# A new issue order for every engine in an attention and mixture-of-experts kernel on one core

## The chip, the core and the metric

The kernel runs on one core of a Trainium2 chip. The metric is device microseconds of one execution, less is better. Times are medians of runs; the trace is of one profiled execution.

## What is computed

The input `x` has 32 sequences of 128 tokens with 128 features. One cross-attention layer and one mixture-of-experts feed-forward layer follow each other. In float32, cut to what matters:

```
xn = layernorm(x); q, k, v = xn@wq+bq, ctx@wk+bk, ctx@wv+bv          # 16 heads of 8
o = (q @ k.T / sqrt(8)) @ v          # linear: no softmax over tokens
x1 = x + softmax(o, over each head's 8 features) @ wo.T + bo
t = rmsnorm(layernorm(x1)) * norm_w
weights = the 2 best of softmax(t @ gate.T) among 8 experts, scaled to sum 1
h1[e] = t@w1.T + 2*(t@a1[e].T)@b1[e].T;  h3[e] the same with w3, a3, b3  # rank 16
act[e] = silu(h1[e]) * h3[e]                                             # 512 wide
out[e] = act[e]@w2.T + 2*(act[e]@a2[e].T)@b2[e].T
result = x1 + sum over the 2 experts of weight * out[e]
```

## The kernel before, in words

**Tiling.** The 32 sequences are cut into 8 blocks (0 to 7, `LAST` is 7) of 4 sequences, 512 tokens. Features lie on the 128 partitions, tokens on the 512 columns. The three stages of the pipeline overlap: while the feed-forward part of block b runs, the attention of block b+2 and the residual, norm and gate of block b+1 are computed between its matmuls, and block b-1 is finished and stored. The 8 experts' low-rank matrices are stacked to 128 rows (8 x 16), and a token's expert is chosen by multiplying with a 0/1 mask, so no token is moved.

**Precision.** Most products of the feed-forward part are split: each operand is a rounded high half (`_hi`, written by ScalarE) and the difference (`_lo`, written by VectorE or GpSimd), and three matmuls (high x high, high x low, low x high) replace one.

**The work of block b, by engine.** TensorE: `hidden(b, n)` for n = 0 to 7 (L628) makes the hidden layer, 128 of its 512 features at a time; even pairs (n = 0, 1, 4, 5) compute the base product (L603) and the first expert's addition (L617) in the two banks h1 and h3, 12 matmuls; the others (2, 3, 6, 7) add the second expert's difference on top, 6 matmuls. The banks are h1[n%2] and h3[n%2] and are free once ScalarE's silu and VectorE's product have read them (L585). `a2_product` (L638) and `w2_product` (L663) are the down projections, 3 matmuls for each of 4 chunks; k=1 accumulates in b_ps from the second expert's activation (`b_split`), k=0 in z_ps from the weighted sum of both (`z_split`). `lora_in(b+1, s)` (L572) makes u for the next block, in the banks h3[0] and h3[1]. `b2_product(b-1)` (L686) and `tail(b-1)` (L696) end the block before. `turn_...` are transposes; with `project`, `queries`, `keys_times_values`, `attention_out` and `gate` they are plain float32.

ScalarE: `silu_step(b, n)`, the high halves (`b_high`, `z_high`, `um_high`, `v_high`, `ctx_high`), the normalisations of x and x1 (`normal_x`, `normal_tok`), copies out of PSUM and the exponentials. silu and exp need different tables, so each block has two table loads.

VectorE: `act_step(b, n)` (L1291, silu x h3, from SBUF and PSUM), residual, moments, softmax pieces (`sum_exp`, L1174), the choice of experts (`top_logits`, `choose`, L1214), then at the end of a block a long run: `scale_last`, `total(2)`, `total(3)`, `b_low` and `z_low` of chunks 2 and 3, the two masks of the next block, `mask_u(b+1, 0)` and `(b+1, 1)` (u x mask, L1276, from PSUM), `um_low(b+1)` (L1286), `first_weight` (L1257: `den`, then a reciprocal), `v_part` twice.

GpSimd: the larger low halves and additions of chunks 0 and 1 (`scale_step`, `total_first`, `b_low`, `z_low`, 1.3 to 2.4 us each), `um_low(b+1)` of the difference (L1608), `norm_heads` (L1601), `scale_mask`, `v_sum`, `v_low`, and the inverse square roots (`rstd_x`, `rstd_x1`, four short operations each with a power in them).

**What sets the order.** Nothing but the written order: each engine has a list of calls for the first block, one for the loop `for b in range(1, LAST)` and one for the last block (L724 on for TensorE, L990 on for ScalarE, L1400 on for VectorE, L1648 on for GpSimd), and every call waits on semaphores for what it needs. Engines execute in order, so a call that waits holds everything behind it. The choice of experts goes through DRAM: `spread_choice` (L399) on the SyncE queue writes `choice` out and reads it back spread over all partitions as `chosen`, on which the masks depend. At the block boundary `hidden(b, 0)` needs, in this order, `um_hi` of the first expert, `um_low(b)` by VectorE for its third lora matmul, and the first of `mask_u(b, 1)` before it may write h3[0].

Lines of work that the change leaves as they are keep all instructions, shapes and buffers; so do the DMA issues of the SyncE queue.

## Time and profile before

| | |
|---|---|
| median of 3 runs | 325.44 us (325.4 to 326.32) |
| the profiled execution | 322.72 us, of which its span is 320.9 us |
| busy: TensorE, VectorE, ScalarE, GpSimd | 92%, 73%, 59%, 59% of the span |
| TensorE clock granted | full speed in 39 of 40 slices, 0.6 in the last |
| start of blocks 1, 2, 3 on TensorE | 69.20, 105.92, 141.82 us |
| start of blocks 6, 7, and the end | 249.51, 283.23, 320.9 us |

A "block" here starts at the first matmul of `hidden(b, 0)` on TensorE. Blocks 2 to 5 take 35.9 us each. Matmul durations in the trace overlap: a 128x512 matmul of a split product lasts 0.39 us but the next starts 0.23 us later, so it is the distance of starts that counts. The median of the timed runs is 2.7 us above the profiled execution.

### The profile page before, as it was taken

How to read it: one execution, taken by the hardware profiler on the slowest of the kernel's cores; microseconds unless marked ns; L12 is line 12 of the kernel's file. 1: busy time of each engine (PE TensorE's matmuls, PEld its weight loads, DVE VectorE, ACT ScalarE, POOL GpSimd, SP SyncE). 2: the span in 40 equal slices, each digit the busy share in tenths (PEclk: the TensorE clock that was granted, in tenths of full speed). 3: DMA queues.
4: the chain of work that ended last, by engine and by line, in shares of the span. 5: the costliest groups of instructions: out<-in, count | busy, mean ns of one | idle time of the engine just before them, and what ended most of it. 6: DMA issues, size and time to landing. Idle time of an engine off the chain costs nothing.

```text
span 320.9 us, 4516 instructions
## 1 busy us (share of the span) xinstructions
PE 294.3 (92%) x1485; PEld 237.1 (74%) x1485; DVE 233.7 (73%) x621; ACT 187.9 (59%) x309; POOL 188.5 (59%) x171
## 2 busy tenths in 40 slices
PE   6768999879999999999999999999999979996993
PEld 5545778658788778878788778878888767885782
DVE  3879877695679766895679767895579766973364
ACT  2456956358657577448657576548647455654511
POOL 3472469727981589527981689527941688136910
PEclk9999999999999999999999999999999999999996
DMA  5720020200201021200211020200010000200000
GB/s 166 260 66 2 1 67 0 100 0 3 98 21 79 0 66 35 99 0 5 96 30 72 0 65 35 99 1 0 35 66 35 0 1 34 102 0 0 33 2 33
DMA packets 7223, 14.50 MB, mean 45 GB/s; under 512 B 1824, under 2 KB 3104, under 8 KB 7200
## 3 DMA queue, kind: packets, MB, share of 16 engines
q1 hardware_dynamic: 6624, 13.62, 12.7%
q10 hardware_dynamic: 576, 0.59, 0.6%
q8 instruction: 12, 0.20, 0.3%
q14 instruction: 11, 0.09, 0.1%
HBM read 12.07 MB, written 2.14 MB: 44 GB/s over the span
## 4 chain that ended last, share of the span: by engine, by line
PE 35%; DVE 24%; POOL 23%; issue 12%; ACT 2%; DMA 2%; ACTq 0%; DVEq 0%; POOLq 0%
PE h_ps L617 15%; PE h_ps L603 6%; POOL um_lo L1608 5%; POOL heads L1601 4%; POOL v_lo L1623 3%; POOL masks L1614 3%; POOL v L1619 3%; DVE act_first L1315 3%; DVE z_lo L1325 3%; DVE scaled L1307 2%; PE odd_ps L692 2%; DVE masks L1239 2%; PE even_ps L452 2%; PE z_ps L452 2%; PE b_ps L452 2%
## 5 line engine op out<-in xcount | busy, mean ns | idle before, releaser
L617 PE MATMUL h_ps<-um_lo,b_hi 128*128 128x512 f32 x128 | 50.9, 398 | 2.3 <-DVE um_lo L1288 2.1
L961 ACT ACTIVATE silu<-h_ps 128x512 f32<-128x512 f32 x64 | 38.2, 597 | 24.7 <-PE h_ps L617 23.3
L617 PE MATMUL h_ps<-um_hi,b_hi 128*128 128x512 f32 x128 | 51.1, 399 | 1.0 <-DVE act_first L1301 0.9
L617 PE MATMUL h_ps<-um_hi,b_lo 128*128 128x512 f32 x128 | 49.9, 390 | 0.0
L1301 DVE TENSOR_TENSOR act_first<-silu,h_ps 128x512 f32<-128x512 f32 x32 | 21.9, 686 | 36.5 <-ACT silu L961 25.2
L1601 POOL TENSOR_TENSOR heads<-e_o,rec_o 128x512 f32<-128x512 f32 (+1 forms) x9 | 14.8, 1642 | 55.9 <-DVE rec_o L1178 55.9
L1630 POOL TENSOR_TENSOR scaled<-act_second,ratio 128x512 f32<-128x512 f32 x24 | 31.0, 1291 | 11.0 <-DVE act_second L1301 10.9
L1301 DVE TENSOR_TENSOR act_second<-silu,h_ps 128x512 f32<-128x512 f32 x32 | 21.6, 679 | 16.9 <-PE h_ps L617 13.4
L617 PEld LDWEIGHTS h_ps<-um_lo,b_hi 128*128 128x128 f32 x128 | 24.0, 188 | 10.4 <-DVE um_lo L1288 4.6
L953 ACT CAST um_hi<-umf 128x1024 fp32r<-128x1024 f32 x14 | 14.7, 1053 | 28.3 <-DVE umf L1282 28.3
L603 PE MATMUL h_ps<-t_hi,w_hi 128*128 128x512 f32 x64 | 28.5, 446 | 0.9 <-DVE e_o L1171 0.3
L617 PEld LDWEIGHTS h_ps<-um_hi,b_hi 128*128 128x128 f32 x128 | 24.0, 188 | 6.9 <-DVE act_first L1301 2.0
L1608 POOL TENSOR_TENSOR um_lo<-umf,um_hi 128x1024 fp32r<-128x1024 f32 x7 | 16.8, 2400 | 19.4 <-ACT um_hi L953 19.4
L972 ACT CAST z_hi<-act_first 128x512 fp32r<-128x512 f32 (+1 forms) x24 | 18.2, 764 | 16.6 <-DVE act_first L1315 11.5
L617 PEld LDWEIGHTS h_ps<-um_hi,b_lo 128*128 128x128 f32 x128 | 24.1, 188 | 4.9
L603 PE MATMUL h_ps<-t_hi,w_lo 128*128 128x512 f32 x64 | 25.2, 393 | 0.0
L603 PE MATMUL h_ps<-t_lo,w_hi 128*128 128x512 f32 x64 | 25.1, 393 | 0.0
L965 ACT CAST b_hi<-act_second 128x512 fp32r<-128x512 f32 (+1 forms) x24 | 18.2, 761 | 5.0 <-DVE act_second L1301 4.7
L1645 POOL TENSOR_TENSOR z_lo<-act_first,z_hi 128x1024 fp32r<-128x1024 f32 x8 | 19.0, 2374 | 2.6 <-ACT z_hi L972 2.6
L1635 POOL TENSOR_TENSOR act_first<-act_first,scaled 128x1024 f32<-128x1024 f32 x8 | 19.2, 2397 | 0.6
L1640 POOL TENSOR_TENSOR b_lo<-act_second,b_hi 128x1024 fp32r<-128x1024 f32 x8 | 19.1, 2383 | 0.0
L1282 DVE SCALAR_TENSOR_TENSOR umf<-h_ps,masks 128x512 f32<-128x512 f32 x28 | 17.9, 682 | 0.2
(275 smaller groups left out, 788.4 us busy)
## 6 DMA issues: line engine op xcount, KB each, us to landing
chosen<-choice_dram SPq DMA_DIRECT2D x7, 768.0 KB, 3.9
x_in<-in_x_dram SPq DMA_DIRECT2D x7, 256.0 KB, 2.9
ctx_in<-in_ctx_t_dram SPq DMA_DIRECT2D x7, 256.0 KB, 3.2
out_dram<-y SPq DMA_DIRECT2D x7, 256.0 KB, 2.0
act_second<-in_hidden_w_dram SPq DMA_DIRECT2D x1, 512.0 KB, 4.3
act_second<-in_lora_w_dram SPq DMA_DIRECT2D x1, 512.0 KB, 5.1
v_parts<-in_down_w_dram SPq DMA_DIRECT2D x1, 512.0 KB, 6.1
attn_sb<-in_attn_w_dram SPq DMA_DIRECT2D x1, 260.5 KB, 5.1
```

The costliest lines, as they stand in the source:

```text
L452: mm = nc.tensor.matmul(dst[:, t * n:(t + 1) * n], stationary(t), moving(t), start=True, stop=True)
L603: nc.tensor.matmul((h1_ps, h3_ps)[s][n % 2][:], w13[w][:, s, c * P:(c + 1) * P], t_split[b % 2][m][:], start=(i == 0), stop=False, skip_gr ...
L617: mm = nc.tensor.matmul((h1_ps, h3_ps)[s][n % 2][:], b13[w][:, s, c * P:(c + 1) * P], um[k][m][:, s, :], start=False, stop=(i == 2), skip_ ...
L961: nc.scalar.activation(silu[:, n % SILU_RING, :], h1_ps[n % 2][:], ACT.Silu).then_inc(silu_done.sem, 1)
L965: nc.scalar.copy(b_split[0][:, PARTS[part], :], act_second[:, PARTS[part], :]).then_inc(b_hi_done.sem, 1)
L1301: nc.vector.tensor_tensor((act_first, act_second)[k][:, c, :], silu[:, n % SILU_RING, :], h3_ps[n % 2][:], ALU.mult).then_inc(act_done.sem, 1)
L1601: nc.gpsimd.tensor_tensor(heads[:].rearrange("p t (h k) -> p (t h) k", k=DK)[:, groups(i)], e_o[:, groups(i)], rec.unsqueeze(2).to_broadca ...
L1608: nc.gpsimd.tensor_tensor(um[1][1][:], umf[1][:], as_f32(um[1][0][:]), ALU.subtract)\
L1630: nc.gpsimd.tensor_tensor(scaled[:, c % 2, :], act_second[:, c, :], ratio[:], ALU.mult)\
L1635: nc.gpsimd.tensor_tensor(act_first[:, 0:2, :], act_first[:, 0:2, :], scaled[:], ALU.add)\
L1640: nc.gpsimd.tensor_tensor(b_split[1][:, PARTS[0], :], act_second[:, PARTS[0], :], as_f32(b_split[0][:, PARTS[0], :]), ALU.subtract).then_i ...
L1645: nc.gpsimd.tensor_tensor(z_split[1][:, PARTS[0], :], act_first[:, PARTS[0], :], as_f32(z_split[0][:, PARTS[0], :]), ALU.subtract).then_in ...
```

## The change

Each engine's list of calls is written in a new order, in the first block, in the loop and in the last block. No call is added or removed, no instruction changes its operands, and every wait is the same condition as before. In the loop:

- TensorE: `turn_x`, `turn_heads`, the two `keys_values`, `b2_product` and `tail` come later among the `hidden` steps, `gate(b+1)` moves behind `hidden(b, 5)`, `lora_in(b+1, 0)` moves ahead and `lora_in(b+1, 1)` behind by one w2 product, and `a2_product(b, 2, 0)` becomes the last product of the block.
- VectorE: `tok_low` goes behind `choose` and step 6; `sum_exp(b+2)` goes from the middle of the final run to its end; both `mask_u(b+1, ...)` stand ahead of `um_low(b+1)`; `finish` goes behind step 4.
- ScalarE: `normal_x(b+2)` goes ahead of `silu_step(b, 0)`, behind `um_high`; `exp_o`, `ctx_high`, `exp_ratio`, `exp_gap` change places.
- GpSimd: `v_sum` goes ahead of `scale_mask`, `scale_step(b, 2)` ahead of the x part, `ctx_low` ahead of `rstd_x`, `um_low` ahead of `norm_heads`.

The order in which a2 and w2 products accumulate follows from the tables at the top. The diff, cut to the tables, the loop, the last block and parts of the first:

```diff
@@ -29,14 +29,14 @@
 SECOND = [STEPS.index((c, 1)) for c in range(CHUNKS)]
 SILU_RING = 4
 
-A2_ORDER = ((0, 1, 2, 3), (0, 1, 2, 3))
-W2_ORDER = (0, 1, 2, 3)
-
-FIRST_A2_ORDER = ((0, 1, 2, 3), (0, 1, 2, 3))
+A2_ORDER = ((0, 1, 3, 2), (0, 1, 2, 3))
+W2_ORDER = (1, 0, 2, 3)
+
+FIRST_A2_ORDER = ((1, 2, 0, 3), (2, 1, 0, 3))
 FIRST_W2_ORDER = (0, 1, 2, 3)
 
-LAST_A2_ORDER = ((0, 1, 2, 3), (0, 1, 2, 3))
-LAST_W2_ORDER = (0, 1, 2, 3)
+LAST_A2_ORDER = ((0, 1, 2, 3), (1, 0, 2, 3))
+LAST_W2_ORDER = (1, 0, 2, 3)
...
-            keys_values(2, 0)
             keys_values(2, 1)
             queries(2)
+            project(1)
+            hidden(0, 2)
+            keys_times_values(2)
+            hidden(0, 3)
             hidden(0, 4)
             turn_tok(1)
-            keys_times_values(2)
+            hidden(0, 5, (1,))
+            gate(1)
             hidden(0, 5, (0,))
-            gate(1)
-            attention_out(2)
-            hidden(0, 5, (1,))
             hidden(0, 6)
             hidden(0, 7)
-            a2_product(0, 0, 1)
-            a2_product(0, 0, 0)
-            a2_product(0, 1, 1)
-            a2_product(0, 1, 0)
+            attention_out(2)
+            lora_in(1, 0)
             w2_product(0, 0)
             w2_product(0, 1)
-            lora_in(1, 0)
             lora_in(1, 1)
             a2_product(0, 2, 1)
+            a2_product(0, 1, 1)
+            a2_product(0, 0, 1)
+            a2_product(0, 1, 0)
             a2_product(0, 2, 0)
             w2_product(0, 2)
             a2_product(0, 3, 1)
+            a2_product(0, 0, 0)
             a2_product(0, 3, 0)
             w2_product(0, 3)
 
             for b in range(1, LAST):
                 early = b + 2 < BLOCKS
                 hidden(b, 0)
+                hidden(b, 1)
+                if early:
+                    turn_x(b + 2)
                 turn_heads(b + 1)
-                hidden(b, 1)
+                if early:
+                    keys_values(b + 2, 0)
+                hidden(b, 2)
                 project(b + 1)
                 if early:
-                    turn_x(b + 2)
-                hidden(b, 2)
+                    keys_values(b + 2, 1)
+                hidden(b, 3)
+                b2_product(b - 1)
+                hidden(b, 4)
+                tail(b - 1)
                 if early:
-                    keys_values(b + 2, 0)
-                b2_product(b - 1)
-                hidden(b, 3)
-                if early:
-                    keys_values(b + 2, 1)
                     queries(b + 2)
-                tail(b - 1)
-                hidden(b, 4)
-                turn_tok(b + 1)
-                if early:
                     keys_times_values(b + 2)
                 hidden(b, 5, (0,))
-                gate(b + 1)
+                turn_tok(b + 1)
                 if early:
                     attention_out(b + 2)
                 hidden(b, 5, (1,))
+                gate(b + 1)
                 hidden(b, 6)
                 hidden(b, 7)
                 a2_product(b, 0, 1)
                 a2_product(b, 0, 0)
+                lora_in(b + 1, 0)
                 a2_product(b, 1, 1)
+                w2_product(b, 1)
+                a2_product(b, 2, 1)
                 a2_product(b, 1, 0)
                 w2_product(b, 0)
-                w2_product(b, 1)
-                lora_in(b + 1, 0)
                 lora_in(b + 1, 1)
-                a2_product(b, 2, 1)
-                a2_product(b, 2, 0)
                 w2_product(b, 2)
                 a2_product(b, 3, 1)
                 a2_product(b, 3, 0)
                 w2_product(b, 3)
+                a2_product(b, 2, 0)
 
             hidden(LAST, 0)
             hidden(LAST, 1)
             hidden(LAST, 2)
+            hidden(LAST, 3)
             b2_product(LAST - 1)
-            hidden(LAST, 3)
-            tail(LAST - 1)
             hidden(LAST, 4)
             hidden(LAST, 5, (0,))
             hidden(LAST, 5, (1,))
             hidden(LAST, 6)
+            tail(LAST - 1)
             hidden(LAST, 7)
-            a2_product(LAST, 0, 1)
             a2_product(LAST, 0, 0)
             a2_product(LAST, 1, 1)
+            w2_product(LAST, 1)
+            a2_product(LAST, 0, 1)
+            a2_product(LAST, 2, 1)
             a2_product(LAST, 1, 0)
-            w2_product(LAST, 0)
-            w2_product(LAST, 1)
-            a2_product(LAST, 2, 1)
             a2_product(LAST, 2, 0)
-            w2_product(LAST, 2)
             a2_product(LAST, 3, 1)
             a2_product(LAST, 3, 0)
+            w2_product(LAST, 0)
+            w2_product(LAST, 2)
             w2_product(LAST, 3)
             last_b2(0)
             last_b2(1)
@@ -992,100 +991,99 @@
             sc.dma_start(rows_sb[:], rows.partition_broadcast(P)).then_inc(rows_in, 16)
...
             for b in range(1, LAST):
                 early = b + 2 < BLOCKS
-                silu_step(b, 0)
-                heads_turned(b + 1)
                 if early:
                     normal_x(b + 2)
+                silu_step(b, 0)
                 silu_step(b, 1)
-                v_high(b - 1)
                 if early:
                     x_turned(b + 2)
+                heads_turned(b + 1)
+                v_high(b - 1)
                 silu_step(b, 2)
+                silu_step(b, 3)
                 output_t(b - 1)
-                silu_step(b, 3)
+                b_high(b, 0)
                 normal_tok(b + 1)
+                silu_step(b, 4)
                 if early:
                     queries(b + 2)
-                b_high(b, 0)
-                silu_step(b, 4)
+                z_high(b, 0)
                 tok_turned(b + 1)
-                z_high(b, 0)
                 silu_step(b, 5)
-                if b + 3 < BLOCKS:
-                    ctx_high(b + 3)
                 silu_step(b, 6)
                 silu_step(b, 7)
                 b_high(b, 1)
                 b_high(b, 2)
                 z_high(b, 1)
                 z_high(b, 2)
-                exp_gap(b + 1)
-                exp_ratio(b + 1)
                 if early:
                     exp_o(b + 2)
+                if b + 3 < BLOCKS:
+                    ctx_high(b + 3)
+                exp_ratio(b + 1)
+                exp_gap(b + 1)
                 um_high(b + 1, 0)
                 um_high(b + 1, 1)
 
...
+            sum_exp(0, 1)
             keys_values(1, 0)
-            sum_exp(0, 1)
+            keys_values(1, 1)
             residual(0, 0)
             moments_x1(0, 0)
-            keys_values(1, 1)
-            first_normalise(tok, x1[0], mv2, rstd2, rstd2_done, tok_done, 0)
             residual(0, 1)
             moments_x1(0, 1)
+            first_normalise(tok, x1[0], mv2, rstd2, rstd2_done, tok_done, 0)
+            mask_ktv(1)
+            round_ident()
             first_normalise(tok, x1[0], mv2, rstd2, rstd2_done, tok_done, 1)
-            mask_ktv(1)
...
             for b in range(1, LAST):
                 early = b + 2 < BLOCKS
                 act_step(b, 0)
+                if early:
+                    keys_values(b + 2, 0)
                 act_step(b, 1)
+                act_step(b, 2)
                 residual(b + 1)
                 moments_x1(b + 1)
-                act_step(b, 2)
-                if early:
-                    keys_values(b + 2, 0)
                 act_step(b, 3)
                 if early:
                     keys_values(b + 2, 1)
-                finish(b - 1)
                 if b + 3 < BLOCKS:
                     moments_x(b + 3)
-                act_step(b, 4)
-                tok_low(b + 1)
                 if early:
                     mask_ktv(b + 2)
-                top_logits(b + 1)
-                choose(b + 1)
-                act_step(b, 5)
+                act_step(b, 4)
+                finish(b - 1)
                 if early:
                     top_of_o(b + 2)
                     shift_o(b + 2)
+                act_step(b, 5)
+                top_logits(b + 1)
+                choose(b + 1)
                 act_step(b, 6)
+                tok_low(b + 1)
                 act_step(b, 7)
+                b_low(b, 1)
                 scale_last(b)
                 total(b, 2)
                 total(b, 3)
-                b_low(b, 1)
                 b_low(b, 2)
                 z_low(b, 1)
+                mask(b + 1, 0)
                 z_low(b, 2)
-                mask(b + 1, 0)
+                mask(b + 1, 1)
                 mask_u(b + 1, 0)
-                mask(b + 1, 1)
-                if early:
-                    sum_exp(b + 2)
+                mask_u(b + 1, 1)
                 um_low(b + 1)
-                mask_u(b + 1, 1)
                 first_weight(b + 1)
                 v_part(b, 0)
                 v_part(b, 1)
+                if early:
+                    sum_exp(b + 2)
 
             act_step(LAST, 0)
             act_step(LAST, 1)
             act_step(LAST, 2)
             act_step(LAST, 3)
-            finish(LAST - 1)
             act_step(LAST, 4)
             act_step(LAST, 5)
             act_step(LAST, 6)
+            finish(LAST - 1)
             act_step(LAST, 7)
+            b_low(LAST, 1)
+            total(LAST, 2)
             scale_last(LAST)
-            total(LAST, 2)
+            z_low(LAST, 1)
             total(LAST, 3)
-            b_low(LAST, 1)
             b_low(LAST, 2)
-            z_low(LAST, 1)
             z_low(LAST, 2)
+            last_part(1, 0)
+            last_part(1, 1)
             last_part(0, 0)
-            last_part(1, 0)
+            last_part(0, 1)
             last_sum(0)
...
@@ -1654,54 +1651,53 @@
             first_rstd_x(0)
             first_rstd_x(1)
             low(WKV, wkv_split, wkv_sb)
+            low(A13, a13, a13_raw)
             rstd_x(1)
-            low(A13, a13, a13_raw)
             norm_heads(0, 0)
             low(W13, w13, w13_raw)
             norm_heads(0, 1)
             first_rstd_x1(0)
             first_rstd_x1(1)
+            ctx_low(2)
+            rstd_x(2)
             low(B13, b13, b13_raw)
-            rstd_x(2)
             norm_heads(1)
-            ctx_low(2)
-
             scale_mask(0)
+            low(B2, b2_split, b2_raw[:])
+            low(W2A2, w2a2, w2a2_raw)
             rstd_x1(1)
-            low(W2A2, w2a2, w2a2_raw)
-            low(B2, b2_split, b2_raw[:])
             scale_step(0, 0)
             scale_step(0, 1)
             total_first(0)
             b_low(0)
             z_low(0)
+            scale_step(0, 2)
             rstd_x(3)
...
             for b in range(1, LAST):
                 early = b + 2 < BLOCKS
+                v_sum(b - 1)
                 scale_mask(b)
-                v_sum(b - 1)
                 v_low(b - 1)
+                scale_step(b, 0)
                 rstd_x1(b + 1)
-                scale_step(b, 0)
                 scale_step(b, 1)
                 total_first(b)
                 b_low(b)
                 z_low(b)
+                scale_step(b, 2)
                 if b + 3 < BLOCKS:
+                    ctx_low(b + 3)
                     rstd_x(b + 3)
-                    ctx_low(b + 3)
-                scale_step(b, 2)
+                um_low(b + 1)
                 if early:
                     norm_heads(b + 2)
-                um_low(b + 1)
-
+
+            v_sum(LAST - 1)
             scale_mask(LAST)
-            v_sum(LAST - 1)
             v_low(LAST - 1)
             scale_step(LAST, 0)
             scale_step(LAST, 1)

```

## Rows read from the trace of the kernel before

**Rows 1.** Stretches by block: length, busy us (instructions) by engine, clock, DMA.

```profile
0.00:69.20 69.20, 57.55 (x308) 44.31 (x309) 52.97 (x169) 39.88 (x74) 36.74 (x51) 1.00 0.24 77
69.20:105.92 36.72, 35.26 (x180) 28.95 (x179) 28.22 (x76) 23.11 (x38) 23.37 (x20) 1.00 0.13 44
105.92:141.82 35.90, 35.29 (x181) 28.95 (x179) 27.43 (x74) 23.07 (x37) 23.41 (x20) 1.00 0.13 45
...
249.51:283.23 33.72, 30.88 (x146) 24.69 (x145) 25.14 (x59) 19.14 (x29) 20.54 (x15) 1.00 0.09 32
283.23:320.90 37.67, 29.50 (x138) 23.36 (x136) 18.82 (x38) 14.05 (x22) 17.09 (x10) 0.93 0.04 14
```

**Rows 2.** TensorE in order of time, block 2 and start of block 3: start, us.

```profile
112.69 1.05 PE L452 MATMUL even_ps<-wo_sb,heads_t 128*128 128x128 f32 x8
113.71 0.63 PE L447 MATMUL z_ps<-query_sb,xn 128*128 128x128 f32 x4
...
116.76 0.47 PE L692 MATMUL odd_ps<-v_hi,b_hi 128*128 128x512 f32 x1 [0.33 <-POOL v_lo L1623]
...
142.72 0.39 PE L617 MATMUL h_ps<-um_hi,b_lo 128*128 128x512 f32 x1
143.32 0.50 PE L617 MATMUL h_ps<-um_lo,b_hi 128*128 128x512 f32 x1 [0.21 <-DVE um_lo L1288]
143.91 0.50 PE L603 MATMUL h_ps<-t_hi,w_hi 128*128 128x512 f32 x1
```

**Rows 3.** VectorE in order of time, block 2 and start of block 3.

```profile
127.39 0.19 DVE L1202 COPY logits<-even_ps 128x32 f32<-128x32 f32 x1 [0.43 <-PE even_ps L452]
...
129.03 0.17 DVE L1226 CAST choice<-top_i 128x8 f32<-128x8 uint32 x1
...
131.78 1.48 DVE L1301 TENSOR_TENSOR act_second<-silu,h_ps 128x512 f32<-128x512 f32 x2
133.36 1.02 DVE L1307 TENSOR_TENSOR scaled<-act_second,ratio 128x512 f32<-128x512 f32 x1
...
140.92 0.68 DVE L1176 TENSOR_REDUCE sum_o<-e_o 128x64 f32<-128x512 f32 x1
...
142.10 1.16 DVE L1288 TENSOR_TENSOR um_lo<-umf,um_hi 128x1024 fp32r<-128x1024 f32 x1
...
144.38 0.16 DVE L1259 TENSOR_SCALAR den<-e_gap 128x4 f32<-128x4 f32 x1
```

**Rows 4.** The SyncE queue in order of time, block 2.

```profile
130.86 0.32 SPq L407 DMA_DIRECT2D chosen<-choice_dram  x1
```

**Rows 5.** DMA issues of the page: KB each, us to landing.

```profile
chosen<-choice_dram SPq DMA_DIRECT2D x7, 768.0 KB, 3.9
```

**Rows 6.** GpSimd in order of time, start of block 3.

```profile
145.62 2.39 POOL L1608 TENSOR_TENSOR um_lo<-umf,um_hi 128x1024 fp32r<-128x1024 f32 x1 [1.43 <-ACT um_hi L953]
```

**Rows 7.** TensorE in order of time, blocks 6 and 7.

```profile
260.36 0.47 PE L692 MATMUL odd_ps<-v_hi,b_hi 128*128 128x512 f32 x1 [1.63 <-POOL v_lo L1623]
...
272.90 0.50 PE L617 MATMUL h_ps<-um_hi,b_hi 128*128 128x512 f32 x1 [0.91 <-DVE act_first L1301]
...
292.74 0.47 PE L692 MATMUL odd_ps<-v_hi,b_hi 128*128 128x512 f32 x1 [2.55 <-POOL v_lo L1623]
```

**Rows 8.** VectorE in order of time, end of block 7.

```profile
304.59 1.64 DVE L1307 TENSOR_TENSOR scaled<-act_second,ratio 128x512 f32<-128x512 f32 x1
...
312.40 0.42 DVE L1375 SCALAR_TENSOR_TENSOR v_parts<-z_ps,masks 128x256 f32<-128x256 f32 x1 [2.55 <-PE z_ps L657]
```

**Rows 9.** VectorE in order of time, block 0.

```profile
22.45 2.62 DVE L1128 TENSOR_SCALAR tok<-x,mv,rstd 128x128 f32<-128x128 f32 x2 [1.08 <-POOL rstd L1570]
...
59.20 0.69 DVE L1307 TENSOR_TENSOR scaled<-act_second,ratio 128x512 f32<-128x512 f32 x1
```

**Rows 10.** GpSimd in order of time, block 0.

```profile
22.39 2.35 POOL L1591 TENSOR_TENSOR b_lo<-act_second,b_hi 128x1024 fp32r<-128x1024 f32 x1
...
58.69 1.02 POOL L1561 TENSOR_TENSOR rstd<-var_eps,minus_half 128x4 f32<-128x4 f32 x1
```

154 lines of the change are left out of this document (74 added, 80 removed).

## The prediction

> **What bounds the kernel now.** I read the stretches first, cut where each block starts on TensorE [rows 1]. Blocks 1 to 6 keep TensorE busy for 31 to 35 us of 34 to 37, all at full clock, VectorE for 25 to 28 and GpSimd for 20 to 23, so the loop belongs to TensorE. Block 0 has 11.7 us without a matmul, block 7 has 8.2, and block 7 alone has a lower clock. Busy time hides short stops, because matmuls overlap, so I then read distances between starts in TensorE's order of time [rows 2]; the normal distance is 0.23. The split lora product at the boundary starts 0.60 after its neighbour (VectorE's `um_low`), and the next matmul 0.59 after it (the h3 bank, freed by `mask_u(b, 1)`, which stands behind `um_low`): with a slow restart 0.84 in all. `b2_product` waits 0.33, with restart 0.45, for `v_low`. The eight matmuls of `project` take about 0.8, the transposes of x begin 1.02 after them, so 0.2 is a wait. Together 1.5 of 35.90: **TensorE's own work in a full block is 34.4 us**. That is the floor that a new order can reach.
>
> VectorE's order of time [rows 3] shows why the boundary waits. From step 7 (second of the two at 131.78, so at 132.57) to the end of `um_low` (143.26) it works without a gap: 10.7 us. Everything from the choice on is such a run, so what counts is which call stands where in it.
>
> **The loop, step by step.**
> Final run of VectorE. `sum_exp` leaves the stretch before `um_low`: 140.92 to 142.10, -1.2. The two umf of `mask_u(b+1, 1)` enter it: they lie between `um_low` and `den` at 144.38, 1.1 to 1.2, +1.2. `scale_last` lasts 1.02 at 133.36, against 0.69 for the same shape elsewhere, as GpSimd is in its own product; it now stands behind `b_low(b, 1)`, when that is over, -0.3. So step 7 to `um_low` takes 10.4. Step 7 starts about 0.3 after TensorE has gone on to what follows `hidden(b, 7)` (an estimate: a matmul lasts 0.16 beyond the next one's start, and a semaphore some 0.1), so `um_low` ends 10.7 after that point. TensorE has 14 groups of three matmuls there (8 a2, 4 w2, 2 lora_in, 0.23 a matmul, 9.6) and asks for `um_low` five matmuls later, at 10.7. Tie: 0 to 0.3 of wait in place of 0.6 + restart, and none for the h3 bank, as both umf are now written earlier. I take 0.15.
> Head of that run. `choose` now follows `gate`, behind step 5; `tok_low` goes between steps 6 and 7. From the copy of the logits to the choice takes 127.39 to 129.20, 1.8 us; with step 6 and `tok_low` (0.6, 0.7) this gives 3.1 from the logits, plus 1.0 for `gate` itself, 4.1, against 0.8 + 2.8 + 0.3 = 3.9 until `hidden(b, 7)` is through. 0.2 late at worst, nothing if the choice is not held up by GpSimd as it is here.
> Choice of experts. Written at 129.20; the read is issued at 130.86 [rows 4] and lands 3.9 later [rows 5], 5.6 in all. In the new order the choice is ready 1.0 + 1.8 - 0.2 = 2.6 after `gate` starts, so `chosen` lands at 8.2; the first mask comes up behind step 7 (at 4.0) and six operations of 0.6, with their small gaps at about 8.3. Also a tie; I take 0.1. The other DMAs keep their order on the queue; x for block b+3 is still asked for when `residual(b+1)` is done, and what reads it works a block ahead of TensorE.
> ScalarE. `normal_x` (1.6) now delays the silu table and `silu_step(b, 0)`; but `um_high` of the difference ends 2.5 us earlier than now, since `mask_u(b, 1)` moved up, so the silu comes no later. The bank it frees is wanted 7 us into the block. `exp_o` and `ctx_high` ahead of `exp_ratio` delay `ratio`, whose first reader is `scale_mask`, 5 us later. Nothing.
> GpSimd. `um_low` now starts about 1 us into a block instead of 3.8 [rows 6], `norm_heads` behind it ends at about 5, `v_low` at 9. `turn_heads` wants the heads at 5.9, `b2_product` wants `v_low` at 11.4. The 0.45 goes. Were these covers gone, each microsecond late would be one of TensorE's.
> `turn_x` at 5.5 needs x normalised by 2.8: the 0.2 goes. `lora_in(b+1, 1)`, one group later, is still 1 us ahead of `mask_u`. The number of changes between float32 and split products on TensorE stays at five.
> **New full block: 34.4 + 0.25 = 34.65. Blocks 2 to 5: 4 x -1.25 = -5.0. Block 1 (36.72): -2.05.** Bounds for what waits: 0, and 1.5 as now.
>
> **Block 6.** TensorE waits 1.63 for `v_low` and 0.91 for the bank that step 5 frees [rows 7]; with restarts and the boundary, 3.5 of 33.72. The first goes as above. The second came from `choose` standing ahead of step 5; it now stands behind, so this goes too. New: 30.2 + 0.2 = 30.4, -3.3. As block 6 has no attention work, `gate` comes 3.5 us sooner relative to GpSimd's `z_low`, and I expect `choose` to be held by it for about 1.4; that shows at the start of block 7.
>
> **Block 7.** `b2_product` waits 2.55 for `v_low` [rows 7]: gone with the earlier `um_low` and one step more ahead of it, -2.6. `scale_last` lasts 1.64 instead of about 0.7 [rows 8] and now stands behind `b_low` and `total`: -0.6. After the last `z_low` TensorE still does z, w, b, z, four groups, 2.9; in the new tables only the last z product needs it, -2.0, and the w products run while VectorE makes `v`. The k=1 halves of `last_part` no longer wait for the z bank: -0.5 of the 8.5 from 312.40 to the end. +1.4 from block 6's choice. Sum **-4.3**; bounds -6 and 0.
>
> **Block 0.** Normalising the second half of the tokens takes 2.62 [rows 9] because GpSimd makes the low half of the lora weights at that time [rows 10]; the new lists put that behind `rstd_x(2)`: -2.0. For the rest I have only TensorE's 11.7 idle, some 4.5 of it before the first x arrives; the new order starts x's chain at once, and in the a2 stretch first does products that wait for nothing. I take 3.0 of the remaining 5 to 6. **-5.0**, bounds 0 and -8. The moved weight cast may also hold `first_gap`, 2 us; this is within the bounds.
>
> **Sum:** -5.0 - 2.05 - 5.0 - 3.3 - 4.3 = -19.7. The profiled execution took 322.72, the median of the runs is 325.44, 2.7 above; I keep that distance. 322.7 - 19.7 = 303.0, so **305.8** for the median.
>
> **VectorE against GpSimd.** The trace shows the two holding each other: the 2.62 above is a tensor_scalar between SBUF tiles that runs on when GpSimd's operation, begun 0.06 earlier, ends. It shows too that this does not hold for each overlap: `scaled`, with both operands in SBUF, takes its usual 0.69 at 59.20, within GpSimd's power at 58.69 to 59.71 [rows 9, 10]. I therefore price GpSimd's power chains at zero. By the Trainium skill ("SBUF — State Buffer", Who interferes with whom) whoever starts first keeps the shared port for the whole instruction; by that rule `um_low`, which meets `rstd_x`'s power for some 0.4 in each block, would make the sum 2.4 us worse.
>
> **Rivals.**
> *The new boundary catches `den`* (0.25). `den`, a tensor_scalar between SBUF tiles, follows `um_low` at once. `um_high` of the difference ends 0.05 to 0.2 after `den` starts in my layout, and GpSimd's `um_low` (2.40 [rows 6]) then starts; now `den` runs at 144.38 [rows 3] and GpSimd at 145.62, well apart. If GpSimd is first, `den` waits 2.4, and with it two `v_part` (1.2), `sum_exp` (1.2) and the heads (1.2): heads at 1.1 + 2.4 + 0.2 + 3.6 = 7.3, wanted at 5.9. 1.4 in each of six blocks, 8.4: 314. Against: `den` is ahead by a hair; for: so is every number here. The same section of the Trainium skill counts tensor_scalar among the operations that take the shared port; the tensor_scalar of [rows 9] agrees.
> *Only the loop and the end gain* (0.10). Block 0 is a chain of single waits, each replaced by the next: 311.
> *`choose` falls into GpSimd's long run* (0.05), the slower side. Its subtraction and its cast each need SBUF twice. In my layout `z_low` ends 2 us before. If GpSimd is over 2.2 us later, the subtraction waits for `b_low` and the cast for `z_low`, 4.8 together, `chosen` and the run to `um_low` are late by that, and a block takes 39.4: +3.5 in blocks 2 to 5, +2.7 in block 1, +1.5 in block 6; -9.3 at the ends remains: 334.
> *The orders move nothing* (0.02): what waits at the boundary is the length of VectorE's run, which stays. 325.
> Forecast 0.58.
>
> **Numbers.** The range runs from 300 (block 0 at -8, no waits) to 316 (`den` with a weaker start). A measurement of this kernel tells 0.3% (1 us) from no change. Faster 0.93 (forecast, `den`, half gain), same 0.02, slower 0.05.
>
> **What would show it.** Right: blocks 2 to 5 start 34.5 to 35 apart; no wait of `b2_product` or the h3 bank behind `um_low`; `den` at 0.16; `v_low` in block 7 no longer ahead of TensorE; block 1 starts at about 64. Wrong: `den` or `choice` lasting over 1 us in each block, `turn_heads` waiting for the heads, masks waiting for `chosen`, or blocks still 35.9 apart with the waits at other places.

## Result and profile after

The changed kernel takes **305.93 us** (median of 4 runs, 304.18 to 310.74) against 325.42 of the kernel before in the same rounds; the ratio is 0.938, 95% interval 0.932 to 0.944. The forecast was 305.8, in a range of 300 to 316. The profiled execution took 304.74, its span is 302.90. Medians here take in every execution; the ratios leave out the slower state of the core, which one of these four was in.

The sum came out; its terms did so less well. "Iteration b" below is the turn of the loop for block b; the choice of experts that it makes, `chosen`, serves block b+1. The stretches by block, to be held against [rows 1] (columns: length; busy us and instructions of TensorE, its weight loads, VectorE, ScalarE, GpSimd; granted clock; DMA share; GB/s):

```profile
0.00:62.71 62.71, 56.02 (x309) 45.18 (x309) 48.23 (x169) 38.42 (x74) 37.31 (x51) 0.97 0.26 85
62.71:97.02 34.31, 34.31 (x181) 28.86 (x180) 26.76 (x73) 22.98 (x37) 24.29 (x20) 1.00 0.14 47
97.02:133.22 36.20, 34.83 (x181) 28.77 (x180) 29.05 (x77) 24.37 (x39) 23.37 (x22) 1.00 0.13 44
133.22:168.80 35.58, 34.60 (x181) 28.85 (x179) 26.73 (x72) 21.79 (x36) 24.75 (x21) 1.00 0.13 46
168.80:204.47 35.67, 34.84 (x181) 28.77 (x179) 28.52 (x77) 24.34 (x39) 22.76 (x21) 1.00 0.13 45
204.47:238.76 34.29, 34.29 (x181) 28.93 (x180) 25.81 (x65) 22.59 (x37) 20.62 (x16) 1.00 0.09 32
238.76:269.88 31.12, 30.16 (x146) 24.77 (x145) 20.66 (x58) 18.11 (x28) 19.73 (x15) 1.00 0.10 35
269.88:302.90 33.02, 28.75 (x138) 22.57 (x136) 19.26 (x39) 14.90 (x23) 17.15 (x10) 0.98 0.05 16
```

Blocks 1 and 5 last 34.3 us and TensorE has no gap in them: that is the floor, forecast as 34.4. Blocks 2, 3 and 4 should be like them and are 0.9 to 1.6 over the forecast of 34.65. Block 0 is 1.5 better than forecast, although it has a stretch at half clock that the profiled execution of before had not.

TensorE at a start of block that goes well (134.12 to 134.58: starts 0.23 apart where [rows 2] had 0.60 and 0.59), at one that does not (98.69, 99.96), and at block 7's `b2_product`, which waited 2.55 in [rows 7]:

```profile
98.69 0.50 PE L617 MATMUL h_ps<-um_hi,b_hi 128*128 128x512 f32 x1 [0.84 <-ACT um_hi L952]
...
99.96 0.50 PE L617 MATMUL h_ps<-um_lo,b_hi 128*128 128x512 f32 x1 [0.53 <-DVE um_lo L1286]
...
134.12 0.39 PE L617 MATMUL h_ps<-um_hi,b_lo 128*128 128x512 f32 x1
134.35 0.39 PE L617 MATMUL h_ps<-um_lo,b_hi 128*128 128x512 f32 x1
134.58 0.40 PE L603 MATMUL h_ps<-t_hi,w_hi 128*128 128x512 f32 x1
...
279.48 0.39 PE L692 MATMUL odd_ps<-v_hi,b_hi 128*128 128x512 f32 x1
```

VectorE in order of time. `tok` lasts 0.57 for two where [rows 9] had 2.62; `scaled` 0.69 where [rows 3, 8] had 1.02 and 1.64; the first mask of iteration 1 waits for `chosen`, and the second mask (1.16 elsewhere) is held for 0.9 by the `ctx_low` that GpSimd began at 94.05, in the fence after it:

```profile
20.53 0.57 DVE L1126 TENSOR_SCALAR tok<-x,mv,rstd 128x128 f32<-128x128 f32 x2
...
93.04 0.71 DVE L1232 TENSOR_SCALAR masks<-chosen,row_expert_sb 128x512 f32<-128x512 f32 x1 [0.98 <-DMA chosen<-choice_dram]
...
94.27 2.10 DVE L1237 SCALAR_TENSOR_TENSOR masks<-chosen,row_expert_sb,masks 128x512 f32<-128x512 f32 x1
...
125.17 0.69 DVE L1305 TENSOR_TENSOR scaled<-act_second,ratio 128x512 f32<-128x512 f32 x1
...
132.87 1.23 DVE L1286 TENSOR_TENSOR um_lo<-umf,um_hi 128x1024 fp32r<-128x1024 f32 x1
134.01 0.17 DVE L1257 TENSOR_SCALAR den<-e_gap 128x4 f32<-128x4 f32 x1
```

GpSimd beside it. `um_lo` starts 0.9 us into block 3 instead of 3.8 [rows 6], and 0.10 behind the start of `den`:

```profile
94.05 1.46 POOL L1592 TENSOR_TENSOR ctx_lo<-ctx_in,ctx_hi 128x512 fp32r<-128x512 f32 x1 [5.57 <-ACT ctx_hi L884]
...
132.04 1.02 POOL L1558 TENSOR_TENSOR rstd<-var_eps,minus_half 128x4 f32<-128x4 f32 x1
133.14 1.02 POOL L1560 TENSOR_TENSOR shift<-neg_mean,rstd 128x4 f32<-128x4 f32 x1
134.11 2.41 POOL L1605 TENSOR_TENSOR um_lo<-umf,um_hi 128x1024 fp32r<-128x1024 f32 x1
```

So the open question was what costs blocks 2 to 4 some 3.5 us together, and the start of block 7 two waits of the same kind. `chosen` took 5.2, 5.6 and 5.3 us to land in iterations 1, 3 and 6 and 3.8 to 4.2 in the others; before it was 3.8 to 4.5 in all (their median is in [rows 5]). The same three iterations are late in a second profile of the changed kernel (e12: 5.6, 6.1 and 6.2), so it is no accident of one execution.

### The profile page after: what moved, and what is told of

It is laid out like the page before. It is cut to its first block and busy times, and to the rows that moved or that the text cites. A ratio compares the mean times of both kernels' runs of the same rounds, so it can differ in the third digit from the quotient of the medians.

```text
span 302.9 us, 4516 instructions
## 1 busy us (share of the span) xinstructions
PE 287.8 (95%) x1485; PEld 236.7 (78%) x1485; DVE 225.0 (74%) x621; ACT 187.5 (62%) x309; POOL 190.0 (63%) x171
## 3 DMA queue, kind: packets, MB, share of 16 engines
HBM read 12.07 MB, written 2.14 MB: 47 GB/s over the span
## 5 line engine op out<-in xcount | busy, mean ns | idle before, releaser
L1592 POOL TENSOR_TENSOR ctx_lo<-ctx_in,ctx_hi 128x512 fp32r<-128x512 f32 x6 | 9.3, 1552 | 29.4 <-ACT ctx_hi L884 29.4
L603 PE MATMUL h_ps<-t_hi,w_hi 128*128 128x512 f32 x64 | 26.5, 413 | 0.0
```

Source lines behind the costliest of these rows:

```text
L603: nc.tensor.matmul((h1_ps, h3_ps)[s][n % 2][:], w13[w][:, s, c * P:(c + 1) * P], t_split[b % 2][m][:], start=(i == 0), stop=False, skip_gr ...
```

## The experiments

### Which list gives what (e1 to e4)

Each kernel takes the new order (and the order tables of its products) in some of block 0, loop and last block, and the old one in the rest:

```diff
 e1  block 0: new   loop: old   last block: old
 e2  block 0: old   loop: new   last block: old
 e3  block 0: old   loop: old   last block: new
 e4  block 0: old   loop: new   last block: new
```

> The lists of block 0 new, loop and last block as before. My theory (the stretches add up): block 1 starts at about 62.7 instead of 69.2, the rest as before, 325.4 - 6.5 = 319. Rival (block 0 only gains what its end hands to the new loop, as the phase at the boundary belongs to the loop): block 1 starts at 62.7 but is longer, 322. As to the clock: if the stop of 3 us at half the clock in block 0 comes from the new list's gaps, it shows here too and the runs spread.

> The loop new, block 0 and last block as before. My theory: blocks 1 to 6 together 207 instead of 214, and block 7 gains the wait for v_low (2.6) too, as that comes from the loop's earlier um_low: 325.4 - 7 - 2.6 = 316. Rival: block 7 gains only by its own list, 318.5.

> Only the lists of block 7 new. My theory: of its 4.7 the 2.6 of v_low belong to the loop and 2 to 3 to its own order of the products, so 325.4 - 2.5 = 323. Rival: all 4.7 by its own list, 320.7.

> The changed kernel with block 0 as before. By addition 305.9 + 6.5 = 312.4; with TensorE at full clock through block 0, and all runs within 0.5 us of each other if the spread of the changed kernel comes from the clock in block 0. If the spread comes from the late arrival of chosen, it stays.

Measured, with the kernel before at 326.91 us on this chip:

| | ratio [interval] | block 0 | blocks 1 to 6 | block 7 |
|---|---|---|---|---|
| before (first profile) | | 69.20 | 214.03 | 37.67 |
| e1 | 0.973 [0.964, 0.983] | 63.45 | 214.22 | 38.03 |
| e2 | 0.973 [0.966, 0.981] | 71.69 | 209.89 | 37.22 |
| e3 | 0.979 [0.972, 0.986] | 71.39 | 214.03 | 32.18 |
| e4 | 0.965 [0.958, 0.972] | 71.36 | 207.81 | 32.98 |
| changed | 0.938 [0.932, 0.944] | 62.71 | 207.17 | 33.02 |

By time e1's theory came out (317.99 against 319), e2 and e3 went to their rivals (318.86 against 318.5, 320.02 against 320.7), and e4 missed its sum by 3 (315.57 against 312.4), as its block 0 is at 71.36.

The parts can be told apart. Block 0 becomes 5.7 to 6.5 shorter, block 7 5.5 by its own list alone, and the loop, forecast at -10.35, gives only 4 to 7. In e3, with the old loop in front of it, `b2_product` of block 7 still waits, but 0.48 instead of 2.55; in e2, with the new loop and the old last list, it waits 1.05 (first e3, then e2):

```profile
294.22 0.47 PE L692 MATMUL odd_ps<-v_hi,b_hi 128*128 128x512 f32 x1 [0.48 <-POOL v_lo L1623]
```

```profile
291.01 0.47 PE L692 MATMUL odd_ps<-v_hi,b_hi 128*128 128x512 f32 x1 [1.05 <-POOL v_lo L1623]
```

So the last list alone (one step more ahead of the product, `v_sum` ahead of `scale_mask`) takes 2.07 of the 2.55 away, and the loop's earlier `um_low` alone takes 1.50. The two overlap, and the wait belongs to neither by itself. Block 0 had a stretch at half clock in e2, e3 and e4 too, with the old list (71.4 to 71.7 instead of 69.2): the new list does not cause it. And `chosen` lands later than 4.7 only in e2 and e4, the two with the new loop.

### The price of a late `chosen` (e5, e6)

e5 moves the low half of the context back, on ScalarE and GpSimd:

```diff
 silu_step(b, 5)
+if b + 3 < BLOCKS: ctx_high(b + 3)
...
 exp_o(b + 2)
-if b + 3 < BLOCKS: ctx_high(b + 3)
...
+rstd_x(b + 3); ctx_low(b + 3)
 scale_step(b, 2)
-ctx_low(b + 3); rstd_x(b + 3)
```

> The changed kernel with one part undone in the loop: ScalarE's ctx_high(b+3) stands behind silu_step(b, 5) again and GpSimd's rstd_x(b+3) and ctx_low(b+3) ahead of scale_step(b, 2). Theory: where chosen lands over 5 us after its issue, GpSimd's ctx_low starts 0.2 ahead of VectorE's next operation between SBUF tiles (a mask or z_low) and holds it for 1.0; moved away, a late landing costs only its own wait. Blocks 2 to 4 then lose 0.5 to 1.0 each where they had waits, at most 2 us in all: about 304 against 306, and no mask or z_low of the second half over 1.3 us. Rival: the price of a late landing is the wait itself (1.0 to 1.6 before the first mask), and VectorE's run ends late with or without ctx_low; waits for um_high, um_low and z_low on TensorE stay as long as now and the time stays within 0.3%. Second rival: ctx_low now falls among b_low and total of VectorE's run and holds one of these in every block: up to +1 a block, 310.

Measured 310.23 us, ratio 0.945 [0.932, 0.957]. Blocks 2 to 5 last 35.67, 35.91, 35.77 and 35.38 (changed: 36.20, 35.58, 35.67, 34.29). No mask or `z_low` is over 1.18, as the theory had it, and block 2 is 0.5 shorter. But the move has a price at an operation that neither theory nor rival had named: in iterations 2 to 4 `ctx_low` now starts 0.09 ahead of the cast of the choice, holds it for 1.05, and `chosen` is issued that much later. VectorE and GpSimd of e5, in order of time:

```profile
161.95 1.23 DVE L1224 CAST choice<-top_i 128x8 f32<-128x8 uint32 x1
...
169.84 0.70 DVE L1232 TENSOR_SCALAR masks<-chosen,row_expert_sb 128x512 f32<-128x512 f32 x1 [1.14 <-DMA chosen<-choice_dram]
```

```profile
161.86 1.29 POOL L1592 TENSOR_TENSOR ctx_lo<-ctx_in,ctx_hi 128x512 fp32r<-128x512 f32 x1
```

This is the mechanism of the rival "`choose` falls into GpSimd's long run" at a third of its size, with +1.1 in block 5, where the changed kernel was at the floor. Blocks 1 to 5 together are only 1.0 longer than in the changed kernel. That the median comes out at the second rival's 310 is luck: in the profiled execution block 0, whose lists are the same in both, lasts 67.46 instead of 62.71, with 13.6 us of it at half clock.

e6 takes the last z product out from behind the mask:

```diff
-mask(b + 1, 0)
 z_low(b, 2)
+mask(b + 1, 0)
```

> The changed kernel with one call moved in the loop: VectorE's z_low(b, 2) ahead of mask(b+1, 0), so that the last z product doesn't stand behind a mask that waits for chosen. Theory: a late chosen costs 0.6 less, and TensorE's wait for z_low (0.98 in block 3 of the changed kernel) is gone; total gain 0.5 to 1.5 us, 305. Rival: on-time blocks lose as umf and um_high come 0.0 to 0.1 later, nothing else, and the time stays within 0.3% as late landings are few.

Measured 303.36 us (300.92 to 309.45), ratio 0.927 [0.917, 0.938], which overlaps the changed kernel's interval. TensorE no longer waits for VectorE's `z_low`. The gain has to be read at equal landings. Block 2, where `chosen` landed after 5.7, lasts 36.09, with waits of 0.71 and 0.53 for `um_high` and `um_low`; the changed kernel's 36.20 came with a landing of 5.2, but in e12, the same kernel again, the landing was 5.6, the waits 1.23 and 0.53, and the block 36.60. So the move gives about 0.5 in a late block, near the 0.6 that it was to give. The larger part of the price stays: blocks 3 and 4 (34.40 and 34.86) are short here because `chosen` had landed after 3.8 and 4.7.

### Undo the end of VectorE's loop (e7)

```diff
-mask_u(b + 1, 1)
+if early: sum_exp(b + 2)
 um_low(b + 1)
+mask_u(b + 1, 1)
 ...
-if early: sum_exp(b + 2)
```

> The changed kernel with the last part of VectorE's loop as it was: sum_exp(b+2) ahead of um_low(b+1) and mask_u(b+1, 1) behind it. Theory (length of VectorE's run up to um_low sets the boundary): sum_exp adds 1.2 and the two umf take 1.2 out, so um_low itself ends when it did; but umf of the difference comes 2.4 later, um_high of it too, the h3 bank is freed behind um_low, and GpSimd's um_low and with it v_low come 2.4 later. TensorE waits about 0.6 for the h3 bank at five or six block starts, and v_low in block 7 comes later by 1 to 2 us but has room: +3 to +4 us, 309 to 310. Rival: the order of these four calls doesn't matter, as TensorE's new order gives um_low five more matmuls of time; within 0.5% of the changed kernel. Second rival: silu of a block's first step, behind um_high on ScalarE, comes late too: over +6 us, 312.

Measured 313.74 us, ratio 0.960 [0.950, 0.969]: +7.8 on the changed kernel by the medians and 7 by the ratios, twice the forecast. In block 5, which nothing else disturbs, it is +0.9 (35.16 against 34.29). The h3 bank costs less than half of the 0.6 that the theory gave it, 0.26 (starts 0.39 and 0.33 apart instead of 0.23); GpSimd's heads, behind a `um_low` that starts 2.3 us later, are waited for 0.34 to 0.38 there and in blocks 3 and 4. Of the surplus 1.5 lies in block 0 (64.21 against 62.71), whose lists are the same in both. Most of the rest comes where the clock falls. At the start of block 2 the late `chosen` and the late `um_high` stop TensorE for 1.18 and 0.53, and right behind them it runs at half clock for 3.4 us, from 101.8 to 105.2 (rows of TensorE in order of time, and the stretch from 102.20 to 105.80, columns as above):

```profile
100.51 0.50 PE L617 MATMUL h_ps<-um_hi,b_hi 128*128 128x512 f32 x1 [1.18 <-ACT um_hi L952]
...
101.77 0.79 PE L617 MATMUL h_ps<-um_lo,b_hi 128*128 128x512 f32 x1 [0.53 <-DVE um_lo L1286]
```

```profile
102.20:105.80 3.60, 3.60 (x10) 2.76 (x10) 2.16 (x6) 2.83 (x6) 1.72 (x1) 0.58 0.00 0
```

Nine matmuls start in this stretch where 0.23 each would give some sixteen; at half clock they start 0.43 apart. Block 2 takes 38.25. In block 6 the clock falls too (0.62 from 266 to 270; 34.08 instead of 31.12), and in e1, with the old last list, right behind the wait of 2.54 for `v_low` (0.60 and 0.54 from 288 to 292; block 7 takes 38.03). But the stops alone do not decide it. The kernel before had 2.55 at the same place [rows 7] and e12 had 1.23 and 0.53 at the start of block 2, and both kept full clock there; what tips it is open. TensorE of e12:

```profile
98.89 0.50 PE L617 MATMUL h_ps<-um_hi,b_hi 128*128 128x512 f32 x1 [1.23 <-ACT um_hi L952]
...
100.15 0.50 PE L617 MATMUL h_ps<-um_lo,b_hi 128*128 128x512 f32 x1 [0.53 <-DVE um_lo L1286]
```

### The choice earlier (e9)

```diff
 # TensorE
+turn_tok(b + 1)
 hidden(b, 5, (0,))
-turn_tok(b + 1)
+gate(b + 1)
 attention_out(b + 2)
 hidden(b, 5, (1,))
-gate(b + 1)
 # VectorE
+top_logits(b + 1); choose(b + 1)
+act_step(b, 5)
 top_of_o(b + 2); shift_o(b + 2)
-act_step(b, 5)
-top_logits(b + 1); choose(b + 1)
 # ScalarE: tok_turned(b + 1) ahead of z_high(b, 0)
```

> The changed kernel with the choice of experts moved up in the loop: TensorE runs turn_tok ahead of both halves of step 5 and gate between them, VectorE runs top_logits and choose ahead of act_step(b, 5), ScalarE turns tok ahead of z_high(b, 0). Theory: late landings of chosen cost only because the choice is written 0.1 to 0.3 us too late for a landing of 5.6; in block 2 gate can start at about 119.0 instead of 120.02 and the choice is written at about 120.9 instead of 122.6, so chosen is issued 1.2 to 1.7 earlier, no first mask waits for it, and blocks 2 to 4 last 34.3 to 34.6: 2 to 3 us less than the changed kernel, 303. Rival: GpSimd's z_low runs from 118.27 to 120.65, and the earlier choice now meets it: its subtraction or cast lasts 0.5 to 2.4 instead of 0.15, act_step(b, 5) comes late by as much, TensorE waits for the bank at hidden(b, 7), and the blocks last as long as now or up to 1 longer, 306 to 310.

Measured 305.84 us, ratio 0.939 [0.932, 0.947]: nothing gained. `chosen` now lands after 3.7 to 4.1 in all seven iterations and no mask waits, so the theory's half is right. Its price is the rival's and one more: the subtraction of the choice lasts 0.54 to 2.14 in the loop beside GpSimd's `z_low`, ending within 0.03 of it, and `gate` waits 0.48 in blocks 1 to 5 for `even_ps`, which `finish` still reads. Blocks 1 to 5 all last 35.1 to 35.5. VectorE, GpSimd and TensorE of e9, in order of time:

```profile
257.23 2.14 DVE L1220 TENSOR_TENSOR choice<-top_l 128x4 f32<-128x4 f32 x1
```

```profile
256.94 2.40 POOL L1642 TENSOR_TENSOR z_lo<-act_first,z_hi 128x1024 fp32r<-128x1024 f32 x1
```

```profile
116.25 1.06 PE L452 MATMUL even_ps<-attn_sb,tok_t 128*128 128x8 f32 x8 [0.48 <-DVE y L1343]
```

### TensorE's last products (e10)

```diff
-LAST_A2_ORDER = ((0, 1, 2, 3), (1, 0, 2, 3)); LAST_W2_ORDER = (1, 0, 2, 3)
+LAST_A2_ORDER = ((0, 1, 2, 3), (0, 1, 2, 3)); LAST_W2_ORDER = (0, 1, 2, 3)
 # and the calls behind hidden(LAST, 7) in the old order
```

> The changed kernel with TensorE's last products of block 7 and their start and stop tables as in the kernel before (a2 and w2 products of chunk 3 in the order b, z, w at the end, the last z product ahead of one w product only); VectorE, ScalarE and GpSimd keep the new lists. The prediction put 2.0 us on this order. Theory as predicted: block 7 lasts 35.0 instead of 33.0. Rival: as the last z_low (294.83) ends only just after TensorE has come to it, the order is worth the products that it moves behind z alone: w2 of chunks 0 and 2, 6 pairs at 0.117 each, 1.4 together. Second rival: half of that, 0.7, as VectorE's parts from z_ps are held by the z bank and not by TensorE's position.

Measured 308.48 us, ratio 0.947 [0.938, 0.955]. The profiled execution (313.65) can't be held against the other as a whole, since 17 us of its block 0 (68.40 instead of 62.71) ran at half clock. From the end of the last `z_low` to the end of the span it is 8.84 instead of 8.08, and the 0.8 are seen in one row of VectorE, where the changed kernel waits 0.29:

```profile
304.13 0.76 DVE L1373 SCALAR_TENSOR_TENSOR v_parts<-b_ps,masks 128x256 f32<-128x256 f32 x2 [1.12 <-PE b_ps L657]
```

Block 7 as a whole took 32.37, 0.7 less than in the changed kernel: block 6 ran partly below full clock (32.64 instead of 31.12), so TensorE came to block 7's start later than `um_high` and had none of the waits of 0.32 and 0.53 there. The total of a block hides the term, the row shows it. The order of the last products is worth 0.8, near the second rival; the forecast had 2.0.

### The clock in block 0 (e8), and both edits together (e11, e12)

```diff
 queries(0, 1)
+10 x matmul(h1_ps[0][:, 0:P], scrap, scrap)
 keys_times_values(0, 1)
+6 x the same
 attention_out(0, 1)
 ...
 keys_values_ahead(1, 1)
+5 x the same
 turn_heads(0, 1)
```

> The changed kernel with 21 idle matmuls on the scratch tile (0.11 us each, results never read) in TensorE's first three gaps of block 0: ten where it waits for VectorE's kv (1.15), six for ktv (0.68), five for GpSimd's heads (0.58). In the changed kernel the granted clock falls from full to half at 25.2 to 28.8 us, which costs TensorE about 1.6. Theory: the stops of TensorE between 11 and 24 us are what the clock falls for; with three of seven filled the fall is gone or comes later, block 0 lasts 61 to 62. Rival: the fall doesn't depend on these gaps; it comes at the same place, and block 0 lasts 62.7 to 63.5, as now or longer by up to 0.3 where fillers stand in the way of a matmul.

Measured 302.34 us (300.67 to 303.32), ratio 0.926 [0.919, 0.933]. In the profile the fillers leave 0.59, 0.34 and 0.30 of the three waits. Block 0 lasts 61.74, as the theory had it, and no slice of the profiled execution is below full clock; the changed kernel has this stretch:

```profile
25.20:28.80 3.60, 3.60 (x14) 2.70 (x14) 3.23 (x22) 2.32 (x6) 3.34 (x6) 0.53 0.00 0
```

> The two edits that gained, in one kernel: the 21 idle matmuls in TensorE's first gaps of block 0 (e8) and VectorE's z_low(b, 2) ahead of mask(b+1, 0) (e6). Theory: they act at different places, one on the granted clock in block 0 and one on the block ends where chosen lands late, so the gains add: no stretch below full clock in block 0, no wait of TensorE for z_low at a block's end, 300.5 to 301.5, and 1.5% below the changed kernel run beside it, with a narrower spread. Rival: the clock falls for a reason that varies from run to run and from chip to chip, e8 had a lucky chip, and this one spreads from 300 to 310 like the others.

> The changed kernel once more, unedited, on the same chip as e11 and in the same rounds, so that the two can be compared. Theory: 304 to 307 with executions up to 311, clock 0.97 to 0.994, as each execution has at least one stretch at half clock in block 0; e11 is below it by 1 to 2%. Rival: on this chip the clock stays full without the fillers, this one lasts 302 to 303, and only e6's 1 us is left between the two.

e11: **301.14 us** (300.14 to 302.18, 6 runs), ratio 0.924 [0.921, 0.927]. e12, the changed kernel beside it: 307.00 us (304.66 to 311.13, 6 runs), ratio 0.938 [0.933, 0.943]. By the ratios e11 is 1.5% below the changed kernel run beside it, which is clear of both intervals, and it is the best here; the medians, with two long executions of e12 in them, put it at 1.9%. The stretches of blocks 2 to 4, first e11, then e12:

```profile
97.18:131.61 34.43, 34.43 (x181) 28.85 (x179) 27.14 (x74) 23.10 (x38) 23.64 (x21) 1.00 0.14 47
131.61:165.98 34.37, 34.37 (x180) 28.85 (x179) 27.15 (x74) 23.10 (x38) 23.65 (x21) 1.00 0.13 47
165.98:200.38 34.40, 34.40 (x181) 28.85 (x180) 27.14 (x74) 23.11 (x38) 23.67 (x21) 1.00 0.14 47
```

```profile
96.81:133.41 36.60, 34.84 (x181) 28.77 (x179) 29.43 (x78) 24.22 (x39) 23.80 (x21) 1.00 0.13 44
133.41:169.35 35.94, 34.61 (x180) 28.77 (x179) 26.79 (x72) 22.03 (x36) 25.09 (x21) 1.00 0.13 45
169.35:205.01 35.66, 34.85 (x181) 28.77 (x179) 28.51 (x76) 24.32 (x39) 22.55 (x20) 1.00 0.14 45
```

The theory of e11 holds in size and only in part in its reasons. Its profiled execution still has the half-clock stretch in block 0; what the fillers may do shows only over the executions: in the ten of e8 and e11 the mean granted clock is 0.991 to 1.0, in the fourteen of the changed kernel (both series) and e6 it is 0.983 or less six times, and those six are the long ones (307.1 to 311.1). Six of fourteen against none of ten is suggestive and no more, and that the filled waits are the reason is not shown. And 5.0 of the 5.9 us between the two profiled spans lie in blocks 2 to 4, where `chosen` landed late in e12 (5.6 and 6.1) and on time in e11 (4.1, 4.1, 3.9). Blocks 1 to 6 take 203.42 in e11, 10.6 less than before, which is the forecast's loop (10.35); the one late landing in it, 5.2 in iteration 5, costs a wait of 0.39. e8 and e11 differ by less than their intervals, so what e6's move adds to the whole stays open.

### Why `chosen` lands late

The bulk of the 144 packets ends at about the same time in each iteration; in the late ones single packets trail for another 1 to 2 us. In iteration 3 of the changed kernel the last ones end at 4.04, 4.28, 4.51, 4.75, 4.98 and 5.22 behind the issue, 0.23 apart, one after the other. That is how the rest of one engine's share would look (144 packets over 16 engines are nine each); the trace does not say which engine carried a packet. The queues of the changed kernel while `chosen` is under way show the difference. Iteration 2 (124.2 to 129.5) and then iteration 3 (158.5 to 164.2); columns: packets, MB, share of 16 engines:

```profile
q1 hardware_dynamic: 144, 0.79, 38.4%
issues: line engine op xcount, KB each, median us to landing
chosen<-choice_dram SPq DMA_DIRECT2D x1, 768.0 KB, 3.8
...
q1 hardware_dynamic: 144, 0.79, 37.9%
q8 instruction: 1, 0.02, 2.2%
issues: line engine op xcount, KB each, median us to landing
chosen<-choice_dram SPq DMA_DIRECT2D x1, 768.0 KB, 5.6
```

In iteration 3 `chosen` and one packet of queue 8 are all that moves, so other data transfers are not the cause. Such a packet of instructions, 16 KB, goes over queue 8 twelve times in an execution, every 17 to 32 us.

Counted over all fourteen profiles, 98 landings: in the 46 without such a packet from 1.5 us before the issue to 5 behind it, `chosen` took 3.7 to 4.3. In the 52 with one it took 3.8 to 6.4, and all 25 above 4.8 are among these, with the packet starting 0.6 to 3.6 behind the issue (below 0.8 and from 2.9 on there are also some on time). Where it starts later than 3.6, or at 0.5 and earlier, they stay at 3.9 to 4.7. In the kernel before the packets start at 3.1 and later or at 0.5: it had the same packets and missed them. In the slowest of the 25 (e4, iteration 6, 6.4) the bulk of the packets is 0.7 or more later than in any other landing as well, for a reason that stays open.

A second queue of instructions, 14, with packets of 8 KB, is not the cause: it has a packet between 3.1 and 5 behind the issue in 15 of the 46, which took 3.8 to 4.2, and in only 6 of the 25.

The Trainium skill ("Runtime: NRT & Kernel Launch", Instruction fetch mechanics) says that each engine has a DMA queue of its own that fetches its program in blocks of 16 KiB, 256 instructions. The trace agrees for TensorE: its 1485 matmuls and 1485 weight loads make 11.6 such blocks, and queue 8 has 12 packets. It shows only two queues of instructions, 8 and 14, and not one for each engine. In e8 and e11, with 42 instructions more at TensorE's start, the first four packets come 2 to 9 us earlier, in both ahead of iteration 1's transfer, which then lands on time (4.2 and 4.1); and in e9 the transfer itself is earlier and all seven land on time.

The coincidence is shown; that the packet delays `chosen`'s on the one engine that carries both is the likely reading, and no run took the packet away.

## Why the prediction was right, and where not

- **Blocks 1 and 5, the floor: right.** 34.3, forecast 34.4 own work and 34.65 in all. `um_low` and the h3 bank are not waited for, nor `v_low`; `turn_heads` too has its heads.
- **Blocks 2 to 4: mechanism right, size wrong.** The step that failed is the choice of experts, "lands 3.9 later" and "Also a tie; I take 0.1". The tie was seen, but its other side was read from a median. With landings of 5.2, 5.6 and 5.3 the first mask of iterations 1, 3 and 6 waits 0.98, 1.61 and 1.16. Behind the first two GpSimd's `ctx_low` has got going, which holds a mask or `z_low` for 0.9 and 1.1 more. Iteration 1 is paid for at the start of block 2 (1.55 over the forecast), iteration 3 at the end of block 3 (0.93 over) and the start of block 4 (1.0 over), iteration 6 at the start of block 7 (waits of 0.32 and 0.53).
- **Block 6: 0.7 over, a step that was not looked at.** ScalarE's `tok_turned` now stands behind `z_high(b, 0)`. Without attention work TensorE is early here and `gate` waits for it, in every kernel with the new loop but e9, which has the two the other way round:

```profile
256.51 1.03 PE L452 MATMUL even_ps<-attn_sb,tok_t 128*128 128x8 f32 x8 [0.96 <-ACT tok_t L910]
```
- **Block 7: -4.65, forecast -4.3, by other terms.** `v_low` -2.55 (forecast -2.6; the last list alone gives 2.07 of it and the loop alone 1.50, as e3 and e2 show); `scale_last` 1.64 to 0.68, -0.96 (-0.6); last products -0.8 (-2.0); from the first part of v to the end 8.50 to 7.78, -0.7 (-0.5). The 1.4 by block 6's choice did not come: `gate` is late by that wait, and the subtraction lasts 0.14. The old end also ran at half clock from 316 on, behind a wait of 2.3 for `v_hi`, which was not in the sum.
- **Block 0: -6.5, forecast -5.0.** The 2.0 of `tok` is as forecast in its row (2.62 to 0.57); no run shows that all of it reaches the length of the block. The rest was taken at 3.0 and is 4.5, and 1.0 to 1.6 more where the clock stays full (61.74 in e8, 61.13 in e9).
- **Power chains at zero: right.** `um_low` starts at 132.87 within GpSimd's power of 132.04 to 133.06 and lasts 1.23, against 1.16 before. The first 0.19 of it lie within the power and cost at most 0.07; the clearer row is the old `scaled`, 0.69 wholly within a power [rows 9, 10]. By the Trainium skill ("SBUF — State Buffer", Who interferes with whom) `um_low` would have been held for those 0.19; the row says no. GpSimd's `shift`, begun within `um_low`, lasts 1.02 instead of 0.20 and ends with it, as that section has it.
- **Rivals.** `den` was not caught: 0.17, begun 0.10 ahead of GpSimd's `um_low`. `choose` was clear of GpSimd's `z_low` by 1.6, but the mechanism is real, 1.05 in e5 and up to 2.0 in e9. "Only the loop and the end gain" and "nothing moves" fall with e1.

Errors of -2.6 in blocks 0, 1, 5 and 7 and +4.2 in blocks 2, 3, 4 and 6 partly cancelled, and left the profiled execution 1.7 above its forecast (304.74 against 303.0). The median is only 0.1 off because a second error took this back: the distance from the profiled execution to the median was kept at 2.7 and is 1.2. That the total is so much closer than its steps is luck. The 0.3% that the prediction took as the spread was also too small: executions of the changed kernel lie between 304.18 and 311.13.

## What to carry to other kernels

Where a transfer is tied with the call that needs it, take its landing from the slowest instances, and look in which queue's company it travels: instruction packets came at nearly the same times in both profiles of the changed kernel (within 2.8 us), and the reorder had moved transfers onto them. A late arrival costs more than its own wait, as it shifts VectorE's run against GpSimd's and a free call becomes a held one; and stops of TensorE of 1 to 2 us can be followed by a stretch at half clock that costs 1.7 more (e7), though equal stops were not in e12. Sum a forecast by place, and test it by place: mixing old and new lists by section took four kernels and showed in which stretch each gain lay and which gains two lists share.
